# Two passages of a graph-attention and transformer kernel reordered, the stacks fetched in 4 KB pieces, and seven TensorE products without a reader

## The chip, the core and the metric

The kernel runs on one core of a Trainium2 chip. A core has TensorE (matrix products and transposes, into PSUM), VectorE (DVE in the profile), ScalarE (ACT), GpSimd (POOL) and the sync engine SP, which here only issues DMAs. The engines run their instruction lists in order and wait for each other on semaphores. The metric is device time in microseconds (us), lower is better.

## What is computed

The input is x of 16 batches, each 256 tokens by 256 features. A graph-attention layer comes first, then a transformer block whose scales and shifts depend on a condition vector. Cut to what matters here:

```python
x = x + relu(graph_attention(x, cond, adj))      # layer 1, two directions, 16 heads
x1 = ln(x) * (scale1 + 1.0) + shift1             # layer 2
qkv = (x1 @ mat_qkv_w.T + qkv_bias).reshape(B, L, 3, H, hd)   # H = 16, hd = 16
q = l2norm(q) * exp(min(scale_mul, log 100));  k = l2norm(k)
probs = softmax(einsum('bhqd,bhkd->bhqk', q, k), axis=-1)
o = einsum('bhqk,bhkd->bhqd', probs, v)
x = x + (o @ proj_w.T + proj_b) * gamma1
x2 = ln(x) * (scale2 + 1.0) + shift2
x = x + (gelu(x2 @ fc1_w.T + fc1_b) @ fc2_w.T + fc2_b) * gamma2
```

## The kernel before

All 16 batches stay in SBUF (x_res). Three stages follow each other: the graph layer, the attention of layer 2, and the feed-forward part (FFN), which works on pairs of batches. The orders of work are written out by hand, one list for each engine; `turns` calls a function `turn` once per step of a software pipeline, and semaphores tie the engines together.

**Attention, one turn.** A turn has up to four batches in work: f (norm, q and k), b (values and row scores), c (column scores, exponentials, values) and d (output). It is cut into ten steps s (SLOTS). TensorE's steps for one batch are:

- `make_qk`: two products 128x512 for each of two token tiles, q and k in front of their bias (L1521). VectorE adds the bias (`take_qk`, L1172), ScalarE squares (L910), VectorE sums over the 16 dimensions of a head (L1178) and makes a first guess of the inverse root (`first_guess`, L1184 to L1190), GpSimd does three Newton steps (`roots`, L747 to L758), VectorE scales (`unit_qk`, L1215, written to `squares`), TensorE transposes (`split_qk`, L1567), ScalarE copies the high part (`high`, L951), VectorE makes the rest (L1232).
- SP writes high part and rest to `parts_dram` (L632, L637) and fetches them back as `q_stack` and `k_stack` (L642): for each of 8 head pairs 16 rows of the high part, 16 of the high part again or of the rest, and so on, 48 rows in all, and once more from row 64 for the other half of the heads. Row 48 of q_stack holds minus the row maximum, row 48 of k_stack ones (L670).
- `row_scores` (L1548) are rough scores from sums of three keys (`key_blocks`, made by GpSimd, L767 to L775, with `row_head` telling which rows belong to a head), of which VectorE takes maxima (`maxima`, L1225). TensorE transposes the maxima (L1555), ScalarE copies them (L923), and SP sends them into q_stack (`max_row`, L627).
- `col_scores` (L1582) are the true scores, eight groups a turn, into banks 6 and 7 of PSUM; ScalarE takes the exponential of each group (L928) before the next may be written. `make_v` (L1531) and `values` (L1596) give the weighted sums.
- The output of batch d: `output_tokens` (L1615), division on VectorE (L1239, L1243), `output_channels` (L1627), ScalarE's copy (L940), `project` (L1634), `gate` and `residual` on VectorE; GpSimd's `bias` (L782) adds to x_res.

In steady state a turn starts with the column scores of step 0, `make_v` and its copy `take_v` are in steps 2 and 3, and the projection is in step 5.

**First passage.** The lists between the graph stage and the first column scores are written out by batch number: batches 0 and 1 get their q and k while the last graph batches finish. Then the loop starts with f = 1: row scores and maxima of batch 0, `make_v(0)`, norm of batch 2, transposed maxima, rows for the gates (L1643), `split_qk(1)`; then the turn with c = 0.

**Second passage.** In the turn with c = 14 VectorE computes the norm of the first FFN pair (`statistics`, `ffn_normalise`), GpSimd its root (`ffn_root`) and the split of the FFN weights (L817, L819); TensorE transposes it (`ffn_norm`, L1688); ScalarE scales it (`ffn_scale`, L986); VectorE splits it (L1324, L1326). In the turn with c = 15 the products of the first FFN steps (`first`, L1703) stand at the steps FIRST_AT. `first(2)` reuses the bank of the values and waits for their last copy.

## Time and profile before

| | |
|---|---|
| Median of three runs | 795.8 us (793.74 to 796.53) |
| The profiled execution | 793.83 us |
| Its span, first to last instruction | 792.0 us |
| TensorE busy | 731.9 us, 92% |
| VectorE, ScalarE, GpSimd busy | 498.2, 443.1, 326.1 us |
| Mean granted TensorE clock | 0.976 of 2.4 GHz |
| Moved by DMA | 79.65 MB, 101 GB/s |

The graph stage takes the time up to about 250 us, attention that to about 590 us, the FFN the rest. The profile names an instruction by engine, line and tiles, out<-in. A product of two f32 operands appears in the rows as two matmuls, so `x4` at L1521 is one `make_qk` of a token tile. The granted clock is a mean: 1.00 is 2.4 GHz, 0.50 is 1.2 GHz, and what lies between is a stretch with some of each. The DMA share of a short stretch can be over 1, since the times of packets overlap.

### The profile page before, as it was taken

The numbers are of one execution on the slowest core, as the hardware profiler recorded it, in microseconds if no ns is written. First come the engines' busy times: TensorE is split into PE (matmuls) and PEld (weight loads), VectorE is DVE, ScalarE is ACT, GpSimd is POOL, SyncE is SP. The second block draws the span as 40 slices with busy tenths as digits, with TensorE's granted clock in tenths as the row PEclk, the third lists the DMA queues.
The fourth block names the chain that finished last, engine by engine and source line by source line (L and its number), as shares of the span: only waits on it lengthen the run. The fifth ranks groups of instructions, "written<-read, shape, count | busy, mean of one in ns | idle before, by whom it ended". The sixth has DMA issues, their size and how long they took to land.

```text
span 792.0 us, 15017 instructions
## 1 busy us (share of the span) xinstructions
PE 731.9 (92%) x4708; PEld 521.5 (66%) x4708; DVE 498.2 (63%) x1037; ACT 443.1 (56%) x733; POOL 326.1 (41%) x563
## 2 busy tenths in 40 slices
PE   4789999999996689999999999998889999999997
PEld 2477788888873345555555555555548888888885
DVE  2168999989999357767676767666425444444432
ACT  0335555555553266666666666666546555556553
POOL 1024655655653445555555555555442302222200
PEclk9999999999999599999999999999989999999999
DMA  8831333333311777776667767666500000000001
GB/s 239 292 98 37 111 94 115 115 94 113 103 32 40 126 133 149 148 147 150 146 147 146 147 147 147 146 147 155 125 14 1 22 19 14 27 27 28 14 27 40
DMA packets 83096, 79.65 MB, mean 101 GB/s; under 512 B 22942, under 2 KB 71710, under 8 KB 83054
## 3 DMA queue, kind: packets, MB, share of 16 engines
q1 hardware_dynamic: 81726, 78.95, 41.6%
q8 instruction: 23, 0.38, 0.2%
q10 hardware_dynamic: 1328, 0.16, 0.1%
q14 instruction: 19, 0.16, 0.1%
HBM read 57.13 MB, written 21.66 MB: 99 GB/s over the span
## 4 chain that ended last, share of the span: by engine, by line
PE 79%; ACT 6%; DVE 6%; issue 3%; DMA 1%; POOL 1%; ACTq 0%; SPq 0%; DVEq 0%; POOLq 0%
PE ps L1703 11%; PE ps L1717 11%; PE ps L1521 7%; PE ps L1439 7%; PE ps L1596 6%; PE ps L1582 6%; PE ps L1634 4%; PE ps L1531 4%; ACT probsT L928 4%; PE ps L1412 4%; PE ps L1430 4%; PE ps L1459 4%; PE ps L1470 3%; PE ps L1615 2%; PE ps L1548 1%
## 5 line engine op out<-in xcount | busy, mean ns | idle before, releaser
L928 ACT ACTIVATE probsT<-ps 128x1024 f32<-128x1024 f32 x128 | 130.5, 1019 | 29.8 <-PE ps L1582 29.5
L1331 DVE TENSOR_TENSOR hidden_low<-hidden,hidden_high 128x512 fp32r<-128x512 f32 x64 | 46.1, 721 | 115.0 <-ACT hidden_high L1024 67.1
L1021 ACT ACTIVATE hidden<-ps,b_fc 128x512 f32<-128x512 f32 x64 | 44.1, 689 | 73.5 <-PE ps L1703 72.5
L1582 PEld LDWEIGHTS ps<-q_stack,k_stack 49*128 49x128 f32 x512 | 39.0, 188 | 65.3 <-ACT probsT L928 35.3
L1582 PE MATMUL ps<-q_stack,k_stack 49*128 49x256 f32 x512 | 65.5, 335 | 11.9 <-ACT probsT L928 6.8
L1596 PE MATMUL ps<-probsT,v_ones 128*32 128x256 f32 x1024 | 69.2, 388 | 5.0 <-ACT probsT L928 4.8
L713 POOL TENSOR_TENSOR scores<-scores,row_max 128x640 f32<-128x640 f32 x32 | 42.4, 1324 | 76.2 <-DVE row_max L1060 76.2
L1225 DVE TENSOR_REDUCE neg_max<-ps 128x4 bf16<-128x344 f32 x128 | 59.5, 506 | 19.6 <-PE ps L1548 19.6
L1521 PE MATMUL ps<-w_qkv,x1T 128*128 128x512 f32 x128 | 65.3, 634 | 0.0
L1439 PE MATMUL ps<-x_res,w_q 128*128 (+1 forms) x256 | 63.7, 394 | 0.0
L1439 PEld LDWEIGHTS ps<-x_res,w_q 128*128 128x128 f32 x256 | 47.4, 194 | 11.1 <-issue 5.5
L862 ACT ACTIVATE weightT<-ps 80x1024 f32<-80x1024 f32 x32 | 32.6, 1019 | 39.3 <-PE ps L1459 39.3
L718 POOL TENSOR_TENSOR scores<-scores,row_inverse 128x640 f32<-128x640 f32 x32 | 40.7, 1273 | 27.6 <-DVE row_inverse L1103 27.5
L1717 PE MATMUL ps<-hidden_low,w_high 128*128 128x512 f32 x128 | 51.0, 398 | 0.0
L1717 PE MATMUL ps<-hidden_high,w_high 128*128 128x512 f32 x128 | 50.5, 394 | 0.0
L1717 PE MATMUL ps<-hidden_high,w_low 128*128 128x512 f32 x128 | 50.2, 392 | 0.0
L850 ACT ACTIVATE scores<-scores 128x640 f32<-128x640 f32 x32 | 23.6, 738 | 44.9 <-POOL scores L713 44.8
L1596 PEld LDWEIGHTS ps<-probsT,v_ones 128*32 128x32 f32 x1024 | 26.9, 110 | 32.0 <-ACT probsT L928 12.7
L1172 DVE TENSOR_TENSOR qk<-ps,bias_qk 128x512 f32<-128x512 f32 x32 | 22.1, 689 | 37.8 <-issue 21.8
L1215 DVE TENSOR_TENSOR squares<-qk,root 128x1024 f32<-128x1024 f32 x16 | 28.4, 1775 | 22.5 <-POOL root L758 22.5
L910 ACT ACTIVATE squares<-qk 128x512 f32<-128x512 f32 x32 | 20.0, 630 | 40.1 <-DVE qk L1172 40.1
L1024 ACT ACTIVATE hidden_high<-hidden 128x512 fp32r<-128x512 f32 x64 | 40.4, 632 | 2.0
(181 smaller groups left out, 1714.2 us busy)
## 6 DMA issues: line engine op xcount, KB each, us to landing
parts_dram<-part_pairs SPq DMA_DIRECT2D x64, 256.0 KB
q_stack<-parts_dram SPq DMA_DIRECT2D x96, 128.0 KB, 5.3
k_stack<-parts_dram SPq DMA_DIRECT2D x96, 128.0 KB, 6.0
adj<-in_adj SPq DMA_DIRECT2D x16, 440.0 KB, 3.4
xT<-in_xT SPq DMA_DIRECT2D x16, 256.0 KB, 2.7
x_res<-in_x SPq DMA_DIRECT2D x16, 256.0 KB, 3.4
x_in<-in_x SPq DMA_DIRECT2D x16, 256.0 KB, 2.8
gate_rows<-rows_dram SPq DMA_DIRECT2D x16, 256.0 KB, 7.0
```

Of the source, the lines that this page charges most:

```text
L713: nc.gpsimd.tensor_tensor(scores[:, par, d], scores[:, par, d], row_max[:, d].unsqueeze(3).broadcast_to([P, T, H, M]), ALU.subtract).then_ ...
L718: nc.gpsimd.tensor_tensor(scores[:, par, d], scores[:, par, d], inverse[:, d].unsqueeze(3).broadcast_to([P, T, H, M]), ALU.mult).then_inc( ...
L928: nc.scalar.activation(probsT[:, s % 4, :], ps[:, COLS:COLS + 2, :].rearrange("p a n -> p (a n)"), ACT.Exp).then_inc(exp_made, 1)
L1021: nc.scalar.activation(hidden[:, s % RAW, :], ps[:, FC1[s % FC1_BANKS], :], ACT.Gelu, bias=b_fc1[:, m:m + 1]).then_inc(gelu_made, 1)
L1225: nc.vector.tensor_reduce(neg_max[:, tt, at:at + 4], ps[:, ROW_BANKS[j], 0:4 * KP].rearrange("p (a g) -> p a g", a=4), AX_X, ALU.max, nega ...
L1331: nc.vector.tensor_tensor(hidden_parts[1][:, s % H_SLOTS, :], hidden[:, s % RAW, :], hidden_parts[0][:, s % H_SLOTS, :], ALU.subtract).the ...
L1439: mm = nc.tensor.matmul(halves(ps, 2 + d)[:, m, :], w_q[:, d, k, m * P:(m + 1) * P], feat_at(f)[:, k, :], start=(k == 0), stop=(k == C2 - 1))
L1521: mm = nc.tensor.matmul(ps[:, qk_bank(f, tt), :], x1T[:, par, k, tt * P:(tt + 1) * P], w_qkv[:, k, 0:2 * F], start=(k == 0), stop=(k == C2 ...
L1582: mm = nc.tensor.matmul(ps[:, COLS + j, kt * N:(kt + 1) * N], k_stack[at, par, s, kt * P:(kt + 1) * P], q_stack[at, par, s, :], start=True ...
L1596: mm = nc.tensor.matmul(halves(ps, PV_BANK)[32 * j:32 * j + 32, hg % 2, :], v_ones[:, par, kt, HT * (place % 2) + place // 2, :], probsT[: ...
L1703: mm = nc.tensor.matmul(ps[:, FC1[s % FC1_BANKS], :], w1_parts[i][:, k, m * P:(m + 1) * P], x2_parts[j][n % 2][:, k, :], start=(k == 0 and ...
L1717: mm = nc.tensor.matmul(ps[:, FC2_BANK + k, :], w2_parts[i][:, m, k * P:(k + 1) * P], hidden_parts[j][:, s % H_SLOTS, :], start=(m == 0 an ...
```

## The change

1. **Layout of the stacks.** q and k are written with the features of four heads interleaved: `take_qk` writes in the order (group of four heads, dimension, head), the sums of squares and `unit_qk` follow. In `parts_dram` four heads then lie side by side for one dimension, so that a fetch takes pieces of 4 x 256 f32 (4 KB, two per row) instead of 1 KB (eight per row). The stores are cut by half of the features: pieces of 1 KB instead of 2 KB. `row_head` follows the layout and is made by VectorE from `ident` in the setup, no longer by GpSimd.
2. **First passage.** `make_v(0)` stands before the loop. `first_guess(1)` and `b_gated` stand behind the first maxima. The ones for k_stack are issued by ScalarE before the loop instead of by SP behind the fetches. `warm(n)` issues n products of `ident` with `w_qkv` into banks 6 and 7, which nobody reads: one behind each of the first three row scores of batch 0, four ahead of the column scores of batch 0.
3. **Second passage.** `make_v(15)` in step 0 and its copy in step 1; statistics, norm, root and transposes of the first FFN pair earlier, within the turn with c = 14; `ffn_scale` in its last two steps; in the turn with c = 15 the projection in step 6 and the two FFN products in steps 2 and 5.

The diff, cut:

```diff
@@ setup, VectorE (taken away from GpSimd) @@
+                    dve.wait_ge(consts_set, 5)
+                    nc.vector.tensor_reduce(row_head[:], ident[:].rearrange("p (q a) -> p a q", a=HT // 2), AX_X, ALU.add).then_inc(row_heads, 1)
+                    dve.wait_ge(row_heads, 1)
+                    nc.vector.tensor_scalar(row_head[:], row_head[:], 1.0 / 3.0, None, ALU.mult).then_inc(row_heads, 1)
@@ stages @@
-    parts_dram = nc.dram_tensor("parts_dram", (2, HT, 2, HD, C2 * N), F32, kind="Internal").ap()
+    parts_dram = nc.dram_tensor("parts_dram", (2, 2, C2, P, N), F32, kind="Internal").ap()
-    FIRST_AT = (4, 6)
+    FIRST_AT = (2, 5)
+    def project_at(c):
+        return 6 if isinstance(c, int) and c == B - 1 else 5
+    def values_made_at(b):
+        return 0 if isinstance(b, int) and b == B - 1 else 2
@@ SP @@
+        def store(par, w, part):
+            return sp.dma_start(parts_dram[w, part].rearrange("c p n -> p c n"), parts[:, par, w, part].bitcast(F32).rearrange("p (c n) -> p c n", c=C2))
-                sp.dma_start(stack[at:at + SLOT, par].bitcast(F32), parts_dram[w, :, part, :, c * N:(c + 1) * N].rearrange("h d n -> d h n")
+                sp.dma_start(stack[at:at + SLOT, par].bitcast(F32).rearrange("d (j a) n -> d j (a n)", j=2),
+                             parts_dram[w, part, c].rearrange("(j d a) n -> d j (a n)", j=2, d=HD)
-                if isinstance(b, int) and b == 0:
-                    key_ones()
@@ GpSimd, turn @@
             if isinstance(c, int) and c == B - 2:
+                ffn_root(0)
                 pool.wait_ge(g["late_weights"], g["LATE"])
                 split(w_fc1, w1_high, w1_low, w1_split)
@@ ScalarE @@
-                if b is not None and s == 3:
+                if b is not None and s == values_made_at(b) + 1:
                     take_v(b, 1 - par)
-                if isinstance(c, int) and c == B - 1 and s == 0:
-                    act.wait_ge(s_mm, GROUPS * B)
-                if isinstance(c, int) and c == B - 1 and s < C2:
-                    ffn_scale(0, (s,))
+                if isinstance(c, int) and c == B - 2 and s >= SLOTS - C2:
+                    act.wait_ge(s_mm, GROUPS * B)
+                    ffn_scale(0, (s - (SLOTS - C2),))
+        act.wait_ge(x_made, B)
+        for c in range(C2):
+            at = HALF * c + KROWS
+            act.dma_start(k_stack[at:at + 1].bitcast(F32).rearrange("o a h n -> o (a h n)").rearrange("o (p e) -> o p e", p=P),
+                          ones_r[:]).then_inc(key_ones_in, 16)
@@ VectorE @@
-            nc.vector.tensor_tensor(qk[:, tt, :], ps[:, qk_bank(f, tt), :], bias_qk[:], ALU.add).then_inc(qk_out, 1)
+            by_head = "p (g a d) -> p g a d"
+            nc.vector.tensor_tensor(qk[:, tt, :].rearrange("p (g d a) -> p g a d", d=HD, a=4), ps[:, qk_bank(f, tt), :].rearrange(by_head, d=HD, a=4),
+                                    bias_qk[:].rearrange(by_head, d=HD, a=4), ALU.add).then_inc(qk_out, 1)
-            nc.vector.tensor_reduce(sum_sq[:, tt * 2 * H:(tt + 1) * 2 * H], squares[:, tt].rearrange("p (h d) -> p h d", d=HD), AX_X,
+            nc.vector.tensor_reduce(sum_sq[:, tt * 2 * H:(tt + 1) * 2 * H], squares[:, tt].rearrange("p (g d a) -> p g a d", d=HD, a=4), AX_X,
+            rows = "p t (g d a) -> p (t g) d a"
+            nc.vector.tensor_tensor(qkn[:].rearrange(rows, d=HD, a=4), qk[:].rearrange(rows, d=HD, a=4),
+                                    root[0][:].rearrange("p (g a) -> p g a", a=4).unsqueeze(2).broadcast_to([P, HH // 4, HD, 4]), ALU.mult).then_inc(qkn_made, 1)
+                if isinstance(f, int) and f == 1 and s == 1:
+                    first_guess(f)
+                    for k in range(C2):
+                        nc.vector.tensor_scalar(b_gated[:, k, :], ada[:, k, :], b_proj[:, k:k + 1], None, ALU.mult).then_inc(gated_bias, 1)
@@ VectorE, before the loop @@
-        first_guess(1)
         dve.wait_ge(x_made, B)
-        for k in range(C2):
-            nc.vector.tensor_scalar(b_gated[:, k, :], ada[:, k, :], b_proj[:, k:k + 1], None, ALU.mult).then_inc(gated_bias, 1)
@@ TensorE @@
+        def warm(times):
+            for j in range(times):
+                nc.tensor.matmul(ps[:, COLS + j % 2, :], ident[:], w_qkv[:, 0, 0:2 * F], start=True, stop=True)
@@ TensorE, turn @@
+                if isinstance(c, int) and c == 0 and s == 0:
+                    pe.wait_ge(key_ones_in, 16 * C2)
+                    pe.wait_ge(wT_out, 2 * B)
+                    warm(4)
                 for n in groups(b, s):
                     row_scores(b, 1 - par, n)
+                    if isinstance(b, int) and b == 0 and n < GROUPS - 1:
+                        warm(1)
-                if isinstance(c, int) and c == B - 1 and s == 0:
-                    ffn_norm(0)
+                if isinstance(c, int) and c == B - 2 and s == 7:
+                    ffn_norm(0)
@@ TensorE, before the loop @@
+        pe.wait_ge(qk_out, FRONT * T)
+        make_v(0, 0)
```

How the order moves. TensorE in the first passage, from the last transposes of the graph stage to the first column scores (`q_stack,k_stack`); `key_blocks,q_short` are the row scores of batch 0. Before:

```order
L1479 MATMUL ps<-ident,mixT 128x128 x4
L1548 MATMUL ps<-key_blocks,q_short 128x344 x4
L1531 MATMUL ps<-w_qkv,x1T 128x256 x4
L1548 MATMUL ps<-key_blocks,q_short 128x344 x2
L1513 MATMUL ps<-ident,x_hat 128x128 x4
L1548 MATMUL ps<-key_blocks,q_short 128x344 x2
L1555 MATMUL ps<-ident_b,neg_max 16x128 x2
L1643 MATMUL ps<-ident,ada 16x128 x2
L1643 MATMUL ps<-ident,b_gated 16x128 x2
L1567 MATMUL ps<-ident,squares 128x128 x8
L1582 MATMUL ps<-q_stack,k_stack 128x256 x4
```

The same place after the change, in two pieces that join, first from the value product of batch 0 to the gate rows:

```order
L1544 MATMUL ps<-w_qkv,x1T 128x256 x4
L1561 MATMUL ps<-key_blocks,q_short 128x344 x2
L1659 MATMUL ps<-w_qkv,ident 128x512
L1561 MATMUL ps<-key_blocks,q_short 128x344 x2
L1659 MATMUL ps<-w_qkv,ident 128x512
L1561 MATMUL ps<-key_blocks,q_short 128x344 x2
L1659 MATMUL ps<-w_qkv,ident 128x512
L1526 MATMUL ps<-ident,x_hat 128x128 x4
L1561 MATMUL ps<-key_blocks,q_short 128x344 x2
L1568 MATMUL ps<-ident_b,neg_max 16x128 x2
L1653 MATMUL ps<-ident,ada 16x128 x2
L1653 MATMUL ps<-ident,b_gated 16x128 x2
```

The value product of batch 0 has moved ahead of all row scores, and a product without a reader (L1659) stands behind each of the first three. Then, on the same engine, from split_qk of batch 1 on:

```order
L1580 MATMUL ps<-ident,squares 128x128 x8
L1659 MATMUL ps<-w_qkv,ident 128x512 x4
L1592 MATMUL ps<-q_stack,k_stack 128x256 x4
L1534 MATMUL ps<-w_qkv,x1T 128x512 x2
L1592 MATMUL ps<-q_stack,k_stack 128x256 x4
```

Four more such products stand directly ahead of the first column scores; what follows is as before.

VectorE at the same place: `sum_sq`, `minus_half` and `root` are the guess of batch 1, `neg_max` the maxima of batch 0. Before:

```order
L1178 TENSOR_REDUCE sum_sq<-squares 128x32 x2
L1184 TENSOR_SCALAR sum_sq<-sum_sq 128x64
L1186 TENSOR_SCALAR minus_half<-sum_sq 128x64
L1188 TENSOR_SCALAR root<-sum_sq 128x64
L1190 TENSOR_SCALAR root<-root 128x64
L1374 TENSOR_SCALAR b_gated<-ada,b_proj 128x16 x2
L402 BN_STATS stats<-x_res 128x6 x2
L408 BN_AGGR mean_var<-stats 128x2 x2
L1225 TENSOR_REDUCE neg_max<-ps 128x4 x4
```

After the change:

```order
L1189 TENSOR_REDUCE sum_sq<-squares 128x32 x2
L403 BN_STATS stats<-x_res 128x6 x2
L409 BN_AGGR mean_var<-stats 128x2 x2
L1237 TENSOR_REDUCE neg_max<-ps 128x4 x2
L1195 TENSOR_SCALAR sum_sq<-sum_sq 128x64
L1197 TENSOR_SCALAR minus_half<-sum_sq 128x64
L1199 TENSOR_SCALAR root<-sum_sq 128x64
L1201 TENSOR_SCALAR root<-root 128x64
L1282 TENSOR_SCALAR b_gated<-ada,b_proj 128x16 x2
L1237 TENSOR_REDUCE neg_max<-ps 128x4 x2
```

The statistics of batch 2 and the first maxima now come ahead of the guess.

TensorE in the turn with c = 15, from the transposes of the first FFN pair (L1688) to the values that stand ahead of the first FFN product. Before:

```order
L1596 MATMUL ps<-probsT,v_ones 32x256 x16
L1688 MATMUL ps<-ident,x_hat_f 128x128 x8
L1582 MATMUL ps<-q_stack,k_stack 128x256 x8
L1615 MATMUL ps<-ident,o_sumsT 128x128 x8
L1582 MATMUL ps<-q_stack,k_stack 128x256 x4
L1627 MATMUL ps<-ident,o_tok 128x128 x4
L1582 MATMUL ps<-q_stack,k_stack 128x256 x4
L1634 MATMUL ps<-w_proj,oT 128x256 x4
L1596 MATMUL ps<-probsT,v_ones 32x256 x8
```

After the change, as far as the first three products of the FFN:

```order
L1708 MATMUL ps<-ident,x_hat_f 128x128 x8
L1606 MATMUL ps<-probsT,v_ones 32x256 x16
L1592 MATMUL ps<-q_stack,k_stack 128x256 x8
L1625 MATMUL ps<-ident,o_sumsT 128x128 x8
L1592 MATMUL ps<-q_stack,k_stack 128x256 x4
L1637 MATMUL ps<-ident,o_tok 128x128 x4
L1723 MATMUL ps<-x_high_even,w_high 128x512
L1723 MATMUL ps<-x_low_even,w_high 128x512
L1723 MATMUL ps<-x_high_even,w_low 128x512
```

The FFN's transposes now stand ahead of batch 14's last values, and the first FFN products follow batch 14's output transposes directly; the projection (L1634) follows five steps later.

## Rows read from the trace of the kernel before

**Rows 1.** Table of stretches: busy us (instructions) by engine, granted clock, DMA share, GB/s
```profile
400.00:440.00 40.00, 38.90 (x312) 22.98 (x310) 28.20 (x63) 27.95 (x41) 21.09 (x46) 1.00 0.71 146
256.00:260.00 4.00, 1.53 (x5) 1.06 (x6) 3.36 (x13) 0.00 (x0) 2.11 (x7) 0.50 0.78 211
268.00:272.00 4.00, 0.24 (x2) 0.00 (x0) 2.04 (x4) 0.62 (x2) 2.96 (x7) 0.50 0.50 54
272.00:276.00 4.00, 3.11 (x7) 1.70 (x8) 0.00 (x0) 1.02 (x1) 0.39 (x1) 0.50 0.34 89
276.00:280.00 4.00, 4.00 (x11) 1.52 (x10) 2.29 (x6) 1.54 (x2) 0.90 (x2) 0.60 0.71 213
```

**Rows 2.** Chain of waits, first passage: start us, us, what it ran through
```profile
255.20 0.95 DVE root L1188
...
257.59 0.83 DVE neg_max L1225 x2
...
258.94 3.53 PE ps L1531 x8
...
266.70 6.06 DMA q_stack<-neg_maxT
...
273.69 3.71 PE ps L1521 x4
...
278.44 2.32 PE ps L1521 x4
...
290.69 0.67 PE ps L1567 x4
```

**Rows 3.** Chain of waits, second passage
```profile
551.65 1.03 ACT probsT L928
...
555.01 3.04 PE ps L1531 x8
...
570.11 1.02 PE ps L1688 x8
...
577.91 3.78 PE ps L1634 x8
581.69 1.64 PE ps L1596 x16
...
592.70 0.60 ACT o_sumsT L934
```

**Rows 4.** TensorE's waits, 310 to 545 us; then the scaling L1215, durations min/median/max
```profile
PE ps L1596 <- ACT probsT L928: 4.1, 12, 0.4
PE ps L1567 <- DVE squares L1215: 2.0, 7, 0.3
...
L1215 DVE TENSOR_TENSOR squares<-qk,root x14: 1224/2282/2352, 289.4 to 544.7; 128x1024 f32<-128x1024 f32 x14
```

**Rows 5.** Timeline: start, us, engine, line, operation [idle before <- releaser]
```profile
254.53 0.32 PE L1548 MATMUL ps<-key_blocks,q_short 64*128 64x344 bf16 x2 [3.10 <-POOL key_blocks L775]
...
262.60 1.18 SPq L670 DMA_DIRECT2D k_stack<-ones_r  x2
...
263.30 0.25 POOL L758 TENSOR_TENSOR root<-root,head_scale 128x32 f32<-128x32 f32 x1
```

**Rows 6.** Stack fetches (L642) to landing, 255 to 275 us; stretches as in rows 1
```profile
DMA to landing us min/median/max: 3.6/6.4/9.9
...
20.00:30.00 10.00, 8.43 (x26) 4.37 (x24) 0.00 (x0) 3.89 (x7) 0.71 (x2) 1.00 1.04 388
262.00:264.00 2.00, 1.47 (x10) 0.61 (x8) 0.94 (x2) 0.70 (x2) 1.23 (x5) 0.97 1.16 137
```

**Rows 7.** Groups of instructions: busy us, mean ns; GpSimd's by shape, then VectorE's
```profile
L728 POOL TENSOR_TENSOR k_blocks<-k_all,head_of_row 128x160 f32<-128x160 f32 x64 | 27.1, 454 | 25.9 <-POOLq L176 25.9
...
L767 POOL TENSOR_TENSOR x_hat<-part_pairs 128x170 f32<-128x170 f32 x16 | 7.9, 492 | 49.2 <-ACT part_pairs L951 49.2
...
L1172 DVE TENSOR_TENSOR qk<-ps,bias_qk 128x512 f32<-128x512 f32 x32 | 22.1, 689 | 37.8 <-issue 21.8
```

33 lines of the change are left out of this document (9 added, 24 removed).

## The prediction

> **What bounds the kernel now.** I read the table of stretches first. Between 400 and 440 us, inside the attention loop, TensorE is busy 38.9 of 40 us at the full clock, so the long loop is bound by TensorE [rows 1]. The same table shows where that is not so: from 256 to 280 us, the passage from the graph stage to attention, TensorE is busy 0.24 of 4 us in one stretch and works at a granted clock of 0.50 in others (1.2 instead of 2.4 GHz) [rows 1]. The chain of waits says what the 24 us are made of: the guess and b_gated ahead of the first maxima, the value product at half clock (3.53 us), then 6.06 us in which the -max row travels to q_stack, then two q/k products at half clock, 3.71 and 2.32 us [rows 2]. In the second passage, from attention to the feed-forward part, the chain alternates between ScalarE's exponentials and TensorE, and again holds slow products: the last values' product with 3.04 us and the projection with 3.78 us [rows 3]. The feed-forward part behind it (about 190 us) and the graph stage ahead are not touched.
>
> Inside the loop I looked at what TensorE waits for between 310 and 545 us: 4.1 us for exponentials and 2.0 us for the scaling of q and k (L1215), in 235 us [rows 4]. A faster transfer has nothing to give there; no wait for a transfer is among them.
>
> **First passage, up to the first column scores (now at 272.89).** Three things must be there: the -max row, the stacks, and TensorE itself.
>
> *Maxima.* make_v(0) goes ahead of the loop. It needs take_qk(1, 1), done at 251.3, and TensorE then idles 3.10 us for key_blocks [rows 5], so its 1.9 us at full clock (half of the 3.53, the clock being 1.00 there) lie in a pause. It leaves the place between the second and the third row scores, where it cost 3.53. On VectorE the first maxima no longer stand behind the guess and b_gated: sums end at 254.3, statistics and moments take 0.92 (0.67 and 0.25), so the maxima start at 255.3 instead of 257.59 and end at 256.2 [rows 2]. The guess follows; its third step, 0.95 us beside GpSimd's memset [rows 2], should fall to 0.2, so guess and b_gated are over at 257.4. Second maxima to 258.3, normalise(2) 0.8, third to 260.1, fourth to 261.7 or, if a product without a reader holds TensorE at half clock (1.9 us instead of 0.95), 263.0. Transpose and copy (0.7) give the row at 262.5 to 263.8; it was 265.95. The copy take_v(0) runs while ScalarE waits anyway.
>
> *Transfers.* Twelve fetches of 128 KB run from 257.0; the last landed 9.9 us after its issue, at 272.0 [rows 6]. They move 137 GB/s at a full DMA share, in 1 KB pieces; loads with longer rows into 128 partitions moved 388 GB/s at a share of 1.04 [rows 6]. That is the upper bound for 4 KB pieces, but these go to 16 partitions. SP issues until 262.6 in any case, and the shortest landing was 3.6, so the stacks are there between 266.2 and (rate unchanged) 271.5. The stores now have 1 KB pieces instead of 2 KB; if that doubles their cost per byte they land up to 2 us later, inside the same bounds. I take 268, nearer to the fast row since the share says that the packets, not the bytes, fill the engines. The ones leave SP's queue (1.18 us, rows 5) for ScalarE's: two issues there, in front of take_v(0), which waits for the memset until 256.1 anyway; nothing late.
>
> The Trainium skill, "DMA: Bandwidth & Descriptors", section "Why small descriptors are slow (HBM only)", puts a fixed cost of about 3 cycles on each packet, beside 32 bytes moved per cycle. An estimate from that page: a 1 KB piece pays 3 of 35 cycles, so 4 KB pieces would save only some 7% and the first column scores could not start before about 271.5. The sum below would then be 9.8 instead of 10.8.
>
> *TensorE.* GpSimd's roots start when the seed is ready, 257.1, and need 4.9 us: 262.0 instead of 263.55 [rows 5]. The scaling (1.22) ends at 263.3 to 264.3, split_qk(1) at 264.5 to 266.3. Then come the four products of warm(4). One costs half of a q/k pair: 0.95 us at full clock (1.91 for two in the loop), 1.86 at half (3.71 / 2). So they end between 268.3 (full clock) and 273.7 (half). If the clock is low when they start it should rise under them, since TensorE is then busy without pause; in 272 to 280 us it took some 6 us of such work to rise (0.50, then a mean of 0.60) [rows 1]. I take 270.5, between an even chance of the full clock and of a rise on the way. That is later than row and stacks: the products now set the start. Gain: 272.9 - 270.5 = **2.4** (bounds -0.8 and 4.5).
>
> *Clock behind it.* The two q/k products take 1.91 each instead of 3.71 and 2.32: 2.2. Two column scores (0.72 to 0.43) and one row score bring 0.9 more: **3.1**. This is not lost again in the turn: its end hangs on the chain take_qk, squares, roots, scaling, which runs 9.9 us from the second take_qk (280.8) to split_qk(2) (290.69, rows 2) on VectorE and GpSimd, whatever the clock. It starts earlier by the whole 5.5. If the clock is still low at 270.5 this term falls to 1.
>
> **Second passage.** Batch 14's turn: make_v(15) moves from step 2 to step 0, where TensorE stood 1.2 us for an exponential of 1.03 us [rows 3]. It costs 1.9 at full clock instead of 3.04, and 0.7 of it juts out of the pause. take_v (0.60) now stands ahead of the second exponential. ffn_norm(0) (1.02 us, between the turns in rows 3) moves into the pause of step 7; its statistics, root (GpSimd, 1.2 us ahead of the weight split, which has 15 us to spare) and normalisation move with it. Step by step the last values end at 569.0; before, values and ffn_norm ended at 571.13. Gain **2.1** (0.5 if the clock falls as it did here).
>
> Batch 15's turn: the projection moves to step 6, and the two feed-forward products (1.6 us each) to steps 2 and 5, into waits for exponentials; the x2 copies on ScalarE stand ahead of the turn, not between exponentials. Laid out with full-clock durations (column scores 0.45, exponential 1.03, transposes 1.02 and 0.6, o_tok 1.1 on VectorE, values 1.0, projection 1.9) the last sums are out 18.1 us after its first column scores; now it is 593.30 - 571.13 = 22.2 [rows 3]. Of the 4.1, 1.9 are the projection's slow clock and 0.6 that of the values behind it. TensorE still has pauses of 1.4, 0.7 and 0.4 us early in the turn, so one fall of the clock is about even; it would cost 2. I take **3.2** (bounds 1 and 4.1).
>
> **Inside the loop: 0.** PE's list is the same. What changes is how VectorE steps: take_qk writes, and the sum of squares reads, every fourth f32 (16 bytes apart). No row of VectorE shows this step. Nearest: GpSimd's L767 reads with a step of 12 bytes and takes 492 ns for 170 elements; L728 takes 454 for 160 without a step [rows 7]. Per element that is 2.9 against 2.8 ns, so I take no cost. Setup: row_head moves to VectorE, which idles there until 9.3 us.
>
> **Sum.** 2.4 + 3.1 + 2.1 + 3.2 = 10.8 us. The profiled execution took 793.83 (span 792.0 and 1.83 around it) and would become 783.0. It lies 2.0 below the median of the three runs, 795.8, so on the median I forecast **785.0**.
>
> **Rivals.**
> *The clock stays low (0.17).* The pauses left over let it fall in both passages, or the four products run at 1.2 GHz. Terms 0, 1, 0.5 and 2: 3.5 us, 792; with one passage spared 789. For it: 0.50 in 272 to 276 us although TensorE worked 3.1 of the 4 [rows 1]. Against: the added and moved products are long and dense.
> *Steps of 16 bytes slow VectorE down (0.10): slower.* Four instructions a turn (689 ns each, rows 7, and sums of the same size) stand in the chain that TensorE already waits for by 0.3 us in 7 of 14 turns [rows 4]. With x us more on each, a turn grows by 4x less at most 0.4. 14 x (4x - 0.4) eats the gain of 10.8 from x = 0.29 on. At half as long again (0.34) it is 13 us more, 798; at double 33 more, 818.
> The Trainium skill, "Advanced Engine Details and Errata", section "SBUF Cachelines", says that accesses which meet a new 16-byte line each time are penalised and that two hits a line are wanted. By that rule this rival would be the forecast; the row of L767, whose 12-byte step also lands on a new line nearly every time, shows no penalty, on another engine.
> *The collision in the loop goes (0.05).* The scaling takes 2282 ns in the median and 1224 at best [rows 4], depending on whether GpSimd's bias starts first. Shifted timing could end the 2.0 us of waits: 783.
>
> **Chances.** Forecast 0.68, with 780 to 789; rivals 0.17, 0.10, 0.05. The range 778 to 792 leaves out the VectorE rival and the worst clock case. 0.3% (2.4 us) is about what a measurement of this kernel can tell from no change. Faster by more 0.86, within 0.04, slower 0.10.
>
> **What would show it.** The start of the first column scores: 270.5 (268 to 272), released by the products before them and no longer by the -max row. Clock 1.00 in the 4 us after it. The fetches' longest landing well under 9.9 us. The two q/k products there 1.9 each. Second passage: values' product 1.9, projection 1.9, the feed-forward's third product 8 to 13 us earlier than 593.35 in absolute time. take_qk and the sums still 0.69 and 0.68; a turn of the loop still 19.8. A longer take_qk, or a loop turn over 20, refutes the forecast at once.

## The result, and the profile after

The changed kernel is slower by 0.6%: 800.25 us, median of five (798.25 to 802.01), against 795.8 us; ratio 1.0058, 95% interval 1.0032 to 1.0083, so a small loss, but clear of the noise. The forecast was 785.0, in a range of 778 to 792. The profiled execution took 800.25 us, its span 798.3. In the experiments below, three executions ran at a lower clock throughout (one each of experiments 1 and 12, one of the kernel before) and are left out of the ratios; without them the medians of 1 and 12 are 791.3 and 785.2 us.

I cut the span at four starts that every kernel has: the last raw scores of the graph stage, the first column scores, `make_v(2)` and `make_v(14)`, twelve turns of the loop apart. `rest` runs from `make_v(14)` to the end and holds the second passage and the feed-forward part. The second line is a further execution of the kernel before (experiment 6).

| us | graph stage | to first column scores | to make_v(2) | 12 turns | rest | span |
|---|---|---|---|---|---|---|
| before | 233.66 | 39.23 | 27.08 | 237.24 | 254.8 | 792.0 |
| before, again | 236.87 | 37.22 | 26.94 | 237.22 | 253.1 | 791.3 |
| after | 234.60 | 36.26 | 27.90 | 246.81 | 252.7 | 798.3 |

The loop takes 9.6 us more, 0.80 a turn, where I had written 0. The first passage (both columns together) is 2.2 or 0.0 us shorter, depending on which execution of the kernel before one takes, and the second 2.1 or 0.3.

The groups of the page that answer [rows 7]: `take_qk` takes 1078 ns instead of 689. The sums of squares are in a view of one line, from 310 to 545 us (durations min/median/max):

```profile
L1182 DVE TENSOR_TENSOR qk<-ps,bias_qk 128x512 f32<-128x512 f32 x32 | 34.5, 1078 | 32.3 <-issue 19.9
...
L1189 DVE TENSOR_REDUCE sum_sq<-squares x23: 1052/1064/1081, 318.2 to 544.0; 128x32 f32<-128x512 f32 x23
L1227 DVE TENSOR_TENSOR squares<-qk,root x11: 1224/1226/2349, 328.4 to 533.6; 128x1024 f32<-128x1024 f32 x11
```

The last line is the scaling, 2282 in the median before [rows 4]: it now mostly escapes GpSimd's `bias`. In the kernel before the two start together in almost every turn of this stretch, and the one that starts second pays: the scaling took 1.23 us and `bias` 2.34 where the scaling was first (387.36 against 387.39 us), 2.35 and 1.28 where `bias` was (406.88 against 406.89). TensorE's waits in the same stretch answer [rows 4]:

```profile
PE ps L1592 <- ACT probsT L933: 6.0, 23, 0.3
PE ps L1606 <- ACT probsT L933: 4.3, 12, 0.4
PE ps L1580 <- DVE squares L1227: 3.3, 5, 0.7
```

The first line is new: 23 products of the column scores wait for an exponential. ScalarE's own timeline shows why (start us, us, and in brackets the idle time before), in one turn of before and of after:

```profile
379.27 0.63 ACT L910 ACTIVATE squares<-qk 128x512 f32<-128x512 f32 x1 [0.96 <-DVE qk L1172]
```
```profile
381.75 0.63 ACT L915 ACTIVATE squares<-qk 128x512 f32<-128x512 f32 x1 [1.31 <-DVE qk L1182]
```

ScalarE works its list in order. It stands at its square until `take_qk` is done, 0.35 us longer than before, with the next exponential queued behind it, and that exponential is what the column scores wait for.

First passage, TensorE's timeline, answering [rows 2, 5]; the first line is from the kernel before, the others from the changed one:

```profile
290.69 1.09 PE L1567 MATMUL ps<-ident,squares 128*128 128x128 f32 x8 [1.34 <-DVE squares L1215]
```
```profile
256.44 0.32 PE L1561 MATMUL ps<-key_blocks,q_short 64*128 64x344 bf16 x2 [0.47 <-POOL key_blocks L781]
...
266.40 1.09 PE L1580 MATMUL ps<-ident,squares 128*128 128x128 f32 x8 [1.20 <-DVE squares L1227]
267.32 3.60 PE L1659 MATMUL ps<-w_qkv,ident 128*128 128x512 f32 x8
270.86 0.50 PE L1592 MATMUL ps<-q_stack,k_stack 49*128 49x256 f32 x4
271.29 1.99 PE L1534 MATMUL ps<-w_qkv,x1T 128*128 128x512 f32 x4
...
286.80 1.97 PE L1580 MATMUL ps<-ident,squares 128*128 128x128 f32 x8 [1.95 <-DVE squares L1227]
288.70 0.80 PE L1592 MATMUL ps<-q_stack,k_stack 49*128 49x256 f32 x4
289.43 3.60 PE L1606 MATMUL ps<-probsT,v_ones 128*32 128x256 f32 x32
```

The column scores start at 270.86 right behind the four products, at full clock, as forecast. But in the same turn TensorE stands 1.95 us for the scaling (1.34 before) and works at half clock behind it: 32 value products take 3.60 us. The table of stretches, answering [rows 1] (busy us of PE, PEld, DVE, ACT and POOL, then granted clock, DMA share, GB/s):

```profile
268.00:272.00 4.00, 4.00 (x13) 1.72 (x12) 1.67 (x4) 0.78 (x2) 3.36 (x7) 1.00 0.37 115
...
288.00:292.00 4.00, 4.00 (x35) 2.07 (x36) 2.04 (x4) 2.22 (x3) 2.44 (x6) 0.50 0.61 202
560.00:580.00 20.00, 16.87 (x146) 10.80 (x146) 10.69 (x28) 13.07 (x19) 11.58 (x15) 0.91 0.79 133
580.00:600.00 20.00, 17.30 (x126) 10.41 (x127) 3.59 (x8) 10.63 (x14) 8.63 (x9) 0.83 0.05 14
```

The transfers of the stacks from 263 to 267 us, to be set beside the 137 GB/s of [rows 6]:

```profile
DMA packets 206, 0.57 MB, mean 141 GB/s; under 512 B 68, under 2 KB 68, under 8 KB 206
```

Two thirds of the packets are now 4 KB long, and the rate is the same. In the second passage [rows 3] the values' product and the projection fell to 1.99 and 2.00 us (in the second profile of the kernel before the values' product takes 1.99 already, the projection 3.78), but other work now stood at half clock, as the middle line shows, a set of transposes that takes 1.1 us at full clock:

```profile
560.36 1.99 PE L1544 MATMUL ps<-w_qkv,x1T 128*128 128x256 f32 x8
...
566.36 1.97 PE L1625 MATMUL ps<-ident,o_sumsT 128*128 128x128 f32 x8
...
594.26 2.00 PE L1644 MATMUL ps<-w_proj,oT 128*128 128x256 f32 x8
```

### The profile page after: what moved, and what is told of

The parts are those of the page before. It is cut to its first block, busy times and chain, and to the rows that moved or that the text cites. A ratio compares the mean times of both kernels' runs of the same rounds, so it can differ in the third digit from the quotient of the medians.

```text
span 798.3 us, 15049 instructions
## 1 busy us (share of the span) xinstructions
PE 738.2 (92%) x4722; PEld 523.5 (66%) x4722; DVE 514.6 (64%) x1039; ACT 443.7 (56%) x733; POOL 327.6 (41%) x561
## 4 chain that ended last, share of the span: by engine, by line
PE 61%; DVE 14%; issue 10%; ACT 6%; POOL 4%; DMA 0%; POOLq 0%; ACTq 0%; DVEq 0%
PE ps L1723 11%; PE ps L1737 11%; PE ps L1452 7%; PE ps L1606 4%; ACT probsT L933 4%; PE ps L1425 4%; PE ps L1443 4%; PE ps L1472 3%; PE ps L1483 3%; PE ps L1592 3%; PE ps L1644 2%; DVE qk L1182 2%; DVE squares L1227 2%; DVE sum_sq L1189 2%; DVE neg_max L1237 2%
## 5 line engine op out<-in xcount | busy, mean ns | idle before, releaser
L1606 PE MATMUL ps<-probsT,v_ones 128*32 128x256 f32 x1024 | 70.9, 397 | 4.7 <-ACT probsT L933 4.6
L1452 PE MATMUL ps<-x_res,w_q 128*128 (+1 forms) x256 | 65.3, 401 | 0.0
L1534 PE MATMUL ps<-w_qkv,x1T 128*128 128x512 f32 x128 | 63.3, 617 | 0.0
L1182 DVE TENSOR_TENSOR qk<-ps,bias_qk 128x512 f32<-128x512 f32 x32 | 34.5, 1078 | 32.3 <-issue 19.9
L1227 DVE TENSOR_TENSOR squares<-qk,root 128x1024 f32<-128x1024 f32 x16 | 26.1, 1633 | 28.9 <-POOL root L764 28.9
L753 POOL TENSOR_TENSOR root_sq<-root 128x64 f32<-128x64 f32 x45 | 13.2, 294 | 75.3 <-DVE root L1201 73.0
```

Source lines behind the costliest of these rows:

```text
L1182: nc.vector.tensor_tensor(qk[:, tt, :].rearrange("p (g d a) -> p g a d", d=HD, a=4), ps[:, qk_bank(f, tt), :].rearrange(by_head, d=HD, a=4 ...
L1452: mm = nc.tensor.matmul(halves(ps, 2 + d)[:, m, :], w_q[:, d, k, m * P:(m + 1) * P], feat_at(f)[:, k, :], start=(k == 0), stop=(k == C2 - 1))
L1534: mm = nc.tensor.matmul(ps[:, qk_bank(f, tt), :], x1T[:, par, k, tt * P:(tt + 1) * P], w_qkv[:, k, 0:2 * F], start=(k == 0), stop=(k == C2 ...
L1606: mm = nc.tensor.matmul(halves(ps, PV_BANK)[32 * j:32 * j + 32, hg % 2, :], v_ones[:, par, kt, HT * (place % 2) + place // 2, :], probsT[: ...
```

## Experiments

Ratios are to the kernel before on the same chip and in the same stretch of time, with 95% intervals. Its medians there were 794.5 us (experiments 1 to 4), 796.0 (6 to 9) and 795.3 (5 and 10 to 12). The ratios are those of the record; the plain quotients of the medians differ from them by up to 0.25%.

**1. The layout undone.** `take_qk`, sums, scaling, stores, fetches and `row_head` as before; passages and products kept.

> The changed kernel with part 1 (the layout of the stacks) undone on every engine: VectorE steps, stores, fetches and row_head as before; both passages and the seven products kept. Theory S (VectorE's 16-byte steps cost the time): take_qk back from 1078 to 689 ns, sums from 1060 to 680, a loop turn 19.8 instead of 20.5 us, time 786 to 790, about 7 below before. Theory P (the new passages shift the phase of the loop or let the clock fall): turns stay at 20.3 to 20.8 and the time stays near 798. Theory T (the transfers of the new layout) gives the same time as S here and is told apart by the next kernels.

Measured: 791.53 us, ratio 0.9950 (0.9928 to 0.9972). `take_qk` 689 ns, twelve turns 237.22 us: the loop is to 0.02 us that of before. The whole loss is in the layout; theory P falls. But the passages alone bring 4 us by the ratio (3 by the medians) and not 10.8, and the time lies above the 786 to 790 that I expected. In the turn of batch 0 TensorE waits for the row again, and the clock falls twice, behind that wait and behind the one for the scaling:

```profile
273.07 0.56 PE L1584 MATMUL ps<-q_stack,k_stack 49*128 49x256 f32 x4 [3.17 <-DMA q_stack<-neg_maxT]
273.56 3.57 PE L1526 MATMUL ps<-w_qkv,x1T 128*128 128x512 f32 x4
...
289.60 1.20 PE L1572 MATMUL ps<-ident,squares 128*128 128x128 f32 x8 [1.35 <-DVE squares L1219]
...
291.45 3.10 PE L1598 MATMUL ps<-probsT,v_ones 128*32 128x256 f32 x32
```

**2. The layout alone.** The kernel before with part 1 of the change.

> The kernel before with part 1 alone. Theory S: take_qk and sums 0.39 us longer each, turn 20.5 us, time 9 to 12 us above the kernel before (805 to 808). Theory P: no change, within 2 us of 795.8. Theory T: also slower, told apart by the next two kernels.

Measured: 808.52 us, ratio 1.0168 (1.0144 to 1.0192); `take_qk` 1080 ns, twelve turns 247.93. That is 13 us more than before by the ratio, somewhat above what was expected: 10.7 in the twelve turns (20.66 us each) and, in the profile, another 3 between the first column scores and `make_v(2)` (30.14 us against 27.08). The layout costs more here than the some 9 us that experiment 1 gets back.

**3. The order comes with the weights.** The q and k columns of the weight and the bias arrive interleaved, so `take_qk` has no step; the sums still read with one, and the transfers are those of the change.

```diff
-        "w_qkvT": np.asarray(L1_cond_mat_qkv_w).T, "b_qkv_q": L1_cond_q_bias, ...
+        "w_qkvT": by_four(np.asarray(L1_cond_mat_qkv_w)).T, "b_qkv_q": by_four(np.asarray(L1_cond_q_bias)), ...
-            nc.vector.tensor_tensor(qk[:, tt, :].rearrange("p (g d a) -> p g a d", d=HD, a=4), ...
+            nc.vector.tensor_tensor(qk[:, tt, :], ps[:, qk_bank(f, tt), :], bias_qk[:], ALU.add).then_inc(qk_out, 1)
```

> The changed kernel, but the q and k columns of the weights and the bias arrive in the interleaved order, so that take_qk reads and writes without a step. Stores, fetches and unit_qk stay as in the changed kernel, and the sums of squares still read with a step of 16 bytes. Theory S, if the write step and the read step cost each on its own: take_qk 0.69, sums 1.06, a turn near 20.1, time 792 to 796. If only the reading in the sums matters for the turn: 798 to 800. Theory T (transfers): 799 to 801, turn 20.5.

Measured: 793.93 us, ratio 0.9986 (0.9972 to 1.0000). Twelve turns 241.87: of the 9.6 us this one write step was 4.9. The transfers are those of the change and the time is not near the 799 to 801 of theory T, so T falls as the explanation of the loss.

```profile
L1181 DVE TENSOR_TENSOR qk<-ps,bias_qk 128x512 f32<-128x512 f32 x32 | 22.2, 695 | 32.2 <-issue 19.8
...
L1187 DVE TENSOR_REDUCE sum_sq<-squares x24: 1043/1136/1164, 317.6 to 541.5; 128x32 f32<-128x512 f32 x24
```

The other 4.6 us are what is left of the layout. Of the instructions that the layout touches, the sums of squares alone are still slower than before (second line, from the view of one line between 310 and 545 us; 676 ns in the median before). No run takes the reading step alone away without another change, and none fetches 4 KB pieces with no step on any engine; against a share of the fetches speaks only that TensorE waits for no transfer in this loop either.

**4. The reading step goes to ScalarE.** As 3, and the square reads interleaved and writes by heads.

```diff
-            nc.scalar.activation(squares[:, tt, :], qk[:, tt, :], ACT.Square).then_inc(sq_made, 1)
+            nc.scalar.activation(squares[:, tt, :].rearrange("p (g a d) -> p g a d", d=HD, a=4), qk[:, tt, :].rearrange("p (g d a) -> p g a d", d=HD, a=4), ACT.Square).then_inc(sq_made, 1)
```

> As the kernel with reordered weight columns, and ScalarE's squares read with a step of 16 bytes and write in the order of heads, so that VectorE's sums read without a step: no VectorE instruction has a step, the transfers are those of the changed kernel. Theory S: 785 to 790 if ScalarE does not mind the step (square as long as before, 0.6 us); 790 to 794 if each square grows by 0.4 us. Theory T: 799 to 801.

Measured: 792.58 us, ratio 0.9961 (0.9943 to 0.9979). The sums are back at 685 ns, but now ScalarE pays for the step:

```profile
L915 ACT ACTIVATE squares<-qk 128x512 f32<-128x512 f32 x32 | 36.0, 1128 | 30.2 <-DVE qk L1182 30.2
```

Twelve turns 242.56, no better than 3: the step's price moved to another engine of the same chain (0.44 us a turn for a square that is 0.50 longer). The median is lower than in 3 although the loop is not; the clock stayed at 1.00 in this profile's second passage (rest 248.7 us).

**5. Single instructions, and three ways to fetch 1 MB.** Behind the end of the kernel before.

```diff
+            probed(nc.vector.tensor_tensor(b, src, a, ALU.add))
+            probed(nc.vector.tensor_tensor(wide(b, 2), plain(src, 2), plain(a, 2), ALU.add))
+            probed(nc.vector.tensor_tensor(wide(b, 4), plain(src, 4), plain(a, 4), ALU.add))
...
+            sp.dma_start(whole[16 * i:16 * i + 16].rearrange("d (h n) -> d h n", n=N), ...
+            sp.dma_start(whole[16 * i:16 * i + 16].rearrange("d (h n) -> d h n", n=4 * N), ...
+            sp.dma_start(whole[:, i * N:(i + 1) * N], ...
```

> The kernel before with single instructions behind its end, whose results nobody reads (so its time means nothing): VectorE adds 512 f32 per partition and writes them with steps of 4, 8, 16 and 32 bytes, or reads one operand with a step of 16; VectorE sums 512 f32 to 32 with the same four steps; ScalarE squares 512 with a reading step of 8 and 16 or a writing step of 16; GpSimd adds 512 plainly, with a reading and with a writing step of 16; then 1 MB is fetched from DRAM three times, in 8 transfers of 128 KB each: into 16 partitions in pieces of 1 KB, into 16 partitions in pieces of 4 KB, into 128 partitions in pieces of 1 KB. Theory S (each access to a new 16-byte stretch is paid): VectorE 0.69 us plainly, half-way at 8 bytes, 1.08 at 16 and the same at 32, whether written or read; sums 0.68 and 1.06; ScalarE 0.63 and 1.13; GpSimd no difference, as its row with a step of 12 bytes had none. Rival (the cost grows with the step on and on): 32 bytes dearer than 16. Transfers: theory R (the few partitions bound the fetch, not the length of its pieces): 16 partitions 120 to 140 GB/s with either piece, 128 partitions over 250 GB/s. Rival (the pieces): 1 KB 130 GB/s in both forms, 4 KB over 200.

Measured, groups with mean ns: VectorE's sum of two operands written with steps of 4, 8, 16 and 32 bytes (L1473 to L1476), one operand read with 16 (L1477); reductions read with 4, 8, 16, 32 (L1478 to L1481); ScalarE plain, reading with 8, reading with 16, writing with 16 (L1083 to L1086); GpSimd plain, reading with 16, writing with 16 (L877 to L879).

```profile
L1476 DVE TENSOR_TENSOR hidden<-ps,hidden 128x512 f32<-128x512 f32 x4 | 4.3, 1075 | 0.1
L1475 DVE TENSOR_TENSOR hidden<-ps,hidden 128x512 f32<-128x512 f32 x4 | 4.2, 1058 | 0.1
L1477 DVE TENSOR_TENSOR hidden<-ps,hidden 128x512 f32<-128x512 f32 x4 | 4.2, 1053 | 0.1
L1480 DVE TENSOR_REDUCE x2T<-hidden 128x32 f32<-128x512 f32 x4 | 4.2, 1048 | 0.1
L1474 DVE TENSOR_TENSOR hidden<-ps,hidden 128x512 f32<-128x512 f32 x4 | 2.8, 691 | 0.1
L1473 DVE TENSOR_TENSOR hidden<-ps,hidden 128x512 f32<-128x512 f32 x4 | 2.8, 688 | 0.1
L1084 ACT ACTIVATE hidden<-hidden 128x512 f32<-128x512 f32 x4 | 2.7, 664 | 0.1
L1085 ACT ACTIVATE hidden<-hidden 128x512 f32<-128x512 f32 x4 | 4.4, 1107 | 0.1
L879 POOL TENSOR_TENSOR hidden<-hidden 128x512 f32<-128x512 f32 x4 | 4.4, 1094 | 0.3
L877 POOL TENSOR_TENSOR hidden<-hidden 128x512 f32<-128x512 f32 x4 | 4.2, 1038 | 84.1 <-ACT hidden L1086 83.8
```

On VectorE a step of 8 bytes is free (691 against 688; I had expected half the price), 16 costs 0.37 us, and 32 hardly more (1075 against 1058). ScalarE behaves nearly alike (629 ns plain, 664 with a step of 8 bytes, 1107 with 16). GpSimd, which needs 1038 ns without a step, pays 4 to 5%. The fetches, in the middle of each set (columns as in the table of stretches; only the last two, DMA share and GB/s, matter):

```profile
856.00:858.00 2.00, 0.00 (x0) 0.00 (x0) 0.00 (x0) 0.00 (x0) 0.00 (x0) 0.50 1.17 129
866.00:868.00 2.00, 0.00 (x0) 0.00 (x0) 0.00 (x0) 0.00 (x0) 0.00 (x0) 0.50 1.05 133
876.00:878.00 2.00, 0.00 (x0) 0.00 (x0) 0.00 (x0) 0.00 (x0) 0.00 (x0) 0.50 0.86 262
```

With transfers into 16 partitions each, 129 GB/s with pieces of 1 KB and 133 with 4 KB; with transfers into 128 partitions, 262 GB/s with pieces of 1 KB. The few partitions bound the fetch, not the pieces (theory R).

**6. The kernel before once more**, unchanged.

> The kernel before, unchanged, for a second profile. In the first profile its graph stage is 1.5 to 2.1 us ahead of that of every changed kernel from its second turn on (the fourth-to-last raw scores at 223.58 against 225.0 to 226.2 us), although no instruction before 230 us differs in the kernel with the old layout. Theory J (this is chance of one execution): the graph stage of this profile lies within the spread of the others, and the span is up to 2 us longer than 792.0. Theory F (the changed kernels are slower there): it repeats 223.6 within 0.2 us.

Measured: one execution, 793.08 us, span 791.3. Its graph stage ends 3.2 us later than in the first profile, later than in any other kernel here. Theory F falls. It is J, scatter between executions, though J had put it within the spread of the others; whether the first profile was taken on the same chip is not on record. The passage behind it is 2.2 us shorter: TensorE waits 2.78 us for the row there instead of 4.65, so the wait takes up part of the late start. A single profile tells the length of the first passage to no better than 2 us.

**7. Halved stores.** As 1, with the stores of the change, and with them its shape of `parts_dram`; the fetches keep 1 KB pieces.

```diff
-                sp.dma_start(parts_dram[w, :, 0], parts[:, par, w, 0].bitcast(F32)).then_inc(parts_out, 16)
+                store(par, w, 0).then_inc(parts_out, 16)
-                ... parts_dram[w, :, part, :, c * N:(c + 1) * N].rearrange("h d n -> d h n")
+                ... parts_dram[w, part, c].rearrange("(h d) n -> d h n", d=HD)
```

> The kernel with the old layout on the engines, both passages and the seven products, but with the stores to parts_dram cut in two halves of the features as in the changed kernel (pieces of 1 KB, and the fetches still in pieces of 1 KB). Theory Q (the queue of transfers bounds the first passage): the stores land after 3.4 us instead of 5.45, SP issues the fetches from about 257.3 instead of 259.3 and the -max row about 264, and the first column scores start near 271 instead of 273.07; time 789 to 790.5, against 791.5 with the old stores. Rival (the products and VectorE bound it, or a later fall of the clock eats it): 791 to 792.

Measured: 788.34 us, ratio 0.9920 (0.9890 to 0.9950). SP's issues, in the kernel of experiment 1 and in this one:

```profile
253.15 1.25 SPq L641 DMA_DIRECT2D parts_dram<-part_pairs  x2
254.44 2.06 SPq L646 DMA_DIRECT2D parts_dram<-part_pairs  x2
259.32 0.82 SPq L651 DMA_DIRECT2D q_stack<-parts_dram  x2
```
```profile
252.09 1.96 SPq L639 DMA_DIRECT2D parts_dram<-part_pairs  x4
255.47 0.84 SPq L654 DMA_DIRECT2D q_stack<-parts_dram  x2
```

From the first store to the first fetch 3.4 us instead of 6.2, and the first column scores start at 271.06, where 271 was expected. The one part of the layout that helps seems to be the store, which I had feared. The intervals of 1 and 7 overlap, so the ratios alone don't show it. The profiles speak for it: from the last raw scores to `make_v(2)` it is 62.1 to 62.3 us in the three with halved stores and four products (7, 8, 9), and 64.2 and 64.5 in the two with whole stores and both passages (1, 10).

**8. The row on ScalarE's queue.** As 7.

> As the kernel with halved stores, and the -max row of batch 0 is sent by ScalarE's queue instead of SP's. Theory Q: the row no longer stands behind twelve fetches in one queue and lands 3 to 4 us after its issue at about 264, as the ones did on ScalarE's queue (3.5 us against 8.8 on SP's); the first column scores then wait for the stacks or the four products and start at 269.5 to 270.5; time 788 to 789.5. Rival (the row is slowed by the DMA engines and not by its queue): landing still 6 to 7 us, no gain over the kernel with halved stores.

Measured: 788.06 us, ratio 0.9921 (0.9890 to 0.9951), no change against 7; TensorE still waits 2.4 us for the row.

```profile
256.10 0.82 SPq L654 DMA_DIRECT2D q_stack<-parts_dram  x2
...
263.62 1.93 ACTq L982 DMA_DIRECT2D q_stack<-neg_maxT  x2
```
```profile
271.84 0.50 PE L1593 MATMUL ps<-q_stack,k_stack 49*128 49x256 f32 x4 [2.43 <-DMA q_stack<-neg_maxT]
```

The row lands when the twelve fetches are through, whichever queue it is in: 8 KB, the second half issued by 265.6 us, and not there before 271.8. The ones, 16 KB issued ahead of the fetches, land in 3.5 us. The rival holds.

**9. An eighth product**, ahead of the transposes of step 6 in the first turn. As 8.

```diff
                 if f is not None and s == 6:
+                    if isinstance(c, int) and c == 0:
+                        ...
+                        nc.tensor.matmul(ps[:, QK_BANK, :], ident[:], w_qkv[:, 0, 0:2 * F], start=True, stop=True)
                     split_qk(f, d)
```

> As the kernel with halved stores and the row on ScalarE's queue, with an eighth product without a reader in the turn of batch 0's column scores, ahead of the transposes of step 6, where TensorE stands 1.35 us. Theory C (a fall of the clock behind that pause, 3.03 us for 32 value products instead of 2.0, eats the gain of the first passage): the clock stays at 1.00 through 292 us and the time falls by another 1 us, to 787 to 788.5. Rival: the clock falls all the same, or the turn is bound by ScalarE, and the time stays within 0.5 us of the kernel without it.

Measured: 785.55 us, ratio 0.9893 (0.9862 to 0.9924). The profiles don't bear out my reason: in 8 the clock did not fall there, and first column scores to `make_v(2)` take 25.79 us in both. The difference of the profiles lies in the second passage (rest 248.6 against 251.6), in which nothing was changed and the clock stayed at 1.00. The intervals of 8 and 9 overlap. That the product helps is not shown.

**10. Without the seven products.** As 1.

> The kernel with the old layout and both passages, without the seven products that nobody reads (against 791.5 with them). Theory C (they hold the clock at 1.00 in 256 to 270 us, but the first column scores wait for the row, which lands when the fetches are through): the first column scores start as late as with them, 37 to 38 us behind the last raw scores, the third row scores and transposes in front of them are at half clock, and the time is 0 to 1.5 us longer. Rival (they hold TensorE up, being in front of the column scores): up to 1 us shorter.

Measured: 790.92 us, ratio 0.9949 (0.9929 to 0.9969), against 0.9950 with them. TensorE works at half clock up to the column scores, and these start 37.65 us behind the last raw scores instead of 37.32: they wait 6.06 us for the row. With the old layout and the old stores, where the row sets the start, the seven products bring nothing that can be measured.

**11. Six products instead of four** ahead of the first column scores. As 9.

> As the kernel with halved stores, the row on ScalarE's queue and the eighth product, with six products instead of four ahead of the first column scores, where TensorE still stands 2.27 us for the row at 270 to 272 us and the clock then falls (q/k product 3.29 instead of 1.91). Theory C: the pause shrinks to 0.4 us, both q/k products there take 1.95, and the time falls by 1.3 us to about 784.3. Rival (the turn is bound by what follows on VectorE and ScalarE): within 0.5 us of 785.5.

Measured: 787.82 us, ratio 0.9910 (0.9882 to 0.9939). The pause ahead of the column scores is 0.70 us, both q/k products behind take 1.98, and to `make_v(2)` it is 24.16 us instead of 25.79: the size was right in the profile, but the median is 2.3 us above that of 9 where 1.3 below was expected. The intervals overlap, so neither a gain nor a loss is shown.

**12. Four more products in the second passage.** As 11.

```diff
+    FILL_AT = ((14, 2), (14, 3), (14, 7), (15, 1))
...
+                if isinstance(c, int) and (c, s) in FILL_AT:
+                    ...
+                    nc.tensor.matmul(ps[:, QK_BANK + 1, :], ident[:], w_qkv[:, 0, 0:2 * F], start=True, stop=True)
```

> As the kernel with six products, and one more product that nobody reads in each of four pauses of about 1 us in the second passage: ahead of the column scores of steps 2, 3 and 7 of batch 14 and of step 1 of batch 15. Theory C (what the second passage lacked, 2.9 us gained instead of 5.3, is a fall of the clock behind those pauses): granted clock 1.00 from 540 to 600 us in the profile, from the values' product of batch 14 to the end 248.5 us, and a median up to 2 us below the kernel without them, with less spread between executions. Rival (the clock falls by chance or for another reason, and each product delays what follows): no gain, or 0.5 to 1 us longer.

Measured: 785.62 us, ratio 0.9886 (0.9849 to 0.9923), the lowest ratio of all, and 1.7% below the changed kernel's.

```profile
540.00:560.00 20.00, 19.58 (x162) 11.88 (x158) 14.57 (x28) 13.43 (x19) 15.53 (x22) 1.00 0.94 149
560.00:580.00 20.00, 18.37 (x149) 10.87 (x148) 4.87 (x11) 13.30 (x18) 8.65 (x9) 1.00 0.20 30
580.00:600.00 20.00, 18.81 (x117) 14.46 (x117) 10.57 (x25) 12.04 (x19) 2.50 (x3) 1.00 0.04 14
```

The clock stays up and the rest takes 248.6 us, as expected. But 9 has the same 248.6 without these products, 11 has 250.1, and the spread of the executions is no smaller (783.85 to 789.43). The intervals of 9, 11 and 12 overlap: that the added products pay is possible, not shown.

All profiles by the same cuts:

| us | to first column scores | to make_v(2) | 12 turns | rest |
|---|---|---|---|---|
| 1 layout undone | 37.32 | 26.86 | 237.22 | 252.1 |
| 2 layout alone | 36.65 | 30.14 | 247.93 | 253.4 |
| 3 by weights | 36.63 | 26.89 | 241.87 | 250.9 |
| 4 square on ScalarE | 36.27 | 27.52 | 242.56 | 248.7 |
| 7 halved stores | 36.36 | 25.73 | 237.24 | 250.7 |
| 8 row moved | 36.52 | 25.79 | 237.22 | 251.6 |
| 9 eighth product | 36.36 | 25.79 | 237.24 | 248.6 |
| 10 no products | 37.65 | 26.87 | 237.20 | 250.0 |
| 11 six products | 36.56 | 24.16 | 237.21 | 250.1 |
| 12 second passage | 36.34 | 24.15 | 237.10 | 248.6 |

## Why the prediction was wrong

The spans add up: against the first profile of before, 0.9 us lost in the graph stage, 3.0 gained up to the first column scores, 0.8 lost behind them, 9.6 lost in the twelve turns, 2.1 gained in the rest, together 6.3 us longer (before rounding) where 10.8 shorter was forecast.

**Inside the loop: 0.** This step failed, and it alone turned the sign: 9.6 us in twelve turns. I had no row of VectorE with this step and took GpSimd's L767. Experiment 5 shows that GpSimd is the wrong witness: it takes 1038 ns for what VectorE does in 688, and pays 4 to 5% for a step of 16 bytes where VectorE pays 53 or 54%. A row of another engine was no bound for this one; the range should have kept both ends, down to the double. The Trainium skill, "Advanced Engine Details and Errata", section "SBUF Cachelines", wants two hits on a 16-byte line. The measurement agrees at every step tried (8 bytes free, 16 and 32 about equally dear) and nearly so on ScalarE. I gave that rule a chance of 0.10 where it deserved to be the forecast.

**The rival's price.** With x at 0.39 the rival asked for 4x less 0.4, 1.16 us a turn; it is 0.80. Experiment 3 splits it: the write step alone is worth 4.9 us, or 0.41 a turn, and what is left of the layout, the reading step by all that the profiles show, the other 4.6, or 0.39. Each is about the 0.39 of one instruction, not of two. That fits a chain in which only the `take_qk` and the sum behind the second q/k product stand, but the scaling's collision also went in the changed kernel (median 1226 ns, my third rival) and not in experiment 3 (mean 1771), nor in experiment 2 (mean 1771), whose twelve turns take 1.1 us more than the changed kernel's. How much of the rival's 1.16 that took away is not shown.

**First passage, start: 2.4.** The number came true in the changed kernel: the start moved from 39.23 to 36.26 us behind the last raw scores, to 270.86 in the trace against 270.5, released by the products. In part that was luck, for two errors cancelled. The transposes ahead of the products were to start 29.6 to 30.6 us behind the last raw scores. They start at 29.63 with the layout undone and at 31.80 in the changed kernel, so the slow steps cost 2.2 us here too. The four products then ran at full clock, 3.60 us, where I had taken a mean of full and half. Also, the second profile of before has 37.22 already, and the row lands with the last fetch. The products set the start in the changed kernel, but what they are worth there was not measured; with the layout undone the row sets it, and they are worth nothing that can be measured (experiment 10).

My two ends for the fetch, 137 and 388 GB/s, were for 16 and for 128 partitions, and I took a value near the wrong one. I had read the full DMA share as a sign that the packets, not the bytes, fill the engines; 4 KB pieces moved 141 GB/s in the kernel (137 before) and 133 by themselves (129). The 271.5 that I gave for pieces 7% cheaper is the value of the unchanged rate: 7% of the 14.5 us from 257.0 would make it 270.5. The stores' worth, 2.8 us between first store and first fetch in experiment 7, I had put down as a possible loss.

**Clock behind it, "not lost again in the turn": 3.1.** This failed too. The two q/k products took 1.99 each as forecast, but from the first column scores to `make_v(2)` the kernel took 27.90 us, not 24.0. The pause for the scaling, 1.34 us before, was 1.95, and behind it the clock fell. The chain had become longer by the same slow instructions, which explains the length of the pause. It does not explain the fall by itself: seven profiles have a pause of 1.33 to 1.37 us at this place, and behind it the clock stayed at 1.00 in three (the first of the kernel before, experiments 7 and 8) and fell in four (the second of the kernel before, experiments 1, 4 and 10; 2.9 to 3.6 us for the 32 value products instead of 2.1). One and the same kernel did both. What decides it stays open. I had excluded a second fall by an argument about the chain only. Where neither fall happens 24.16 is reached (experiment 11), so the size was right for a turn at full clock.

**Second passage: 5.3** (2.1 and 3.2). The work moved as planned, but the clock fell in two stretches (0.91 and 0.83 of full speed). Part of what the 2.1 counted on, the values' product at half clock, was chance: the second profile of before does not have it. Against the two profiles of before, 254.8 and 253.1, the rest takes 252.7 in the changed kernel, 250.0 to 252.1 in five profiles with the layout's steps undone, and 248.6 or 248.7 in the three in which the clock holds (4, 9 and 12). From the first profile to that last value it is 6.2 us, from the second 4.5: the sum was that of the good case. The lower bounds, 0.5 and 1, were there; I should have taken the middle.

**The clock rival** (0.17, 789 to 792) describes what the passages did: with the layout undone 791.5. It could not show in the changed kernel, whose loss in the loop it does not hold.

## To carry to other kernels

Before an access pattern changes on an engine, time that one instruction on that engine with that step; a neighbour engine's row is no evidence. The price counts in full where another engine already waits for the chain in which the instruction stands. Ask first whether few partitions bound a fetch: here longer pieces did not speed it up. A gain from a higher clock counts only if the pauses behind it are looked at as well. And a gain of 2 us in a passage needs more than one profile on each side, for two executions of one kernel differed by as much.
